# When TensorE reads a tile's expert number, and where VectorE builds the mixer's weights, in a macaron mixture-of-experts and mamba kernel

## The reference, cut to what matters

```
x = x + 0.5 * ffn(layernorm(x))          # x: 16 x 256 tokens of 128
x = x + attn(layernorm(x))
x = x + 0.5 * ffn(layernorm(x))

ffn(x):                                   # 8 experts, top 2, D = 128, H = 512
    probs = softmax(x @ gate_w); vals, idx = top_k(probs, 2); vals /= sum(vals)
    out = sum over e of combine[:, e] * (silu(x @ w1s[e]) @ w2s[e])

attn(x):
    x1 = x + mamba(rmsnorm(x, norm1_w))
    out2 = mamba(rmsnorm(x1, norm2_w))
    return x1 + memory_attend(out2)       # decayed causal reads, chunk 64

mamba(x):                                 # d_inner 256, conv 4, state 16, dt rank 64
    xm, res = split(x @ in_w.T + in_b)
    xm = silu(causal depthwise conv(xm) + conv_b)
    delta, B, C from xm; h = h * exp(delta * A) + delta * xm * B;  y = h . C
    return ((y + xm * D) * silu(res)) @ out_w.T + out_b
```

## Time and profile before

| | us |
|---|---|
| median of 3 runs (1718.62 to 1725.28) | 1719.58 |
| the profiled execution | 1717.3 |
| its span, first to last instruction | 1715.5 |
| TensorE busy (matmul) | 1330.5, 78% |
| VectorE busy | 1379.7, 80% |
| ScalarE busy | 1278.6, 75% |
| GpSimd busy | 568.3, 33% |
| mean granted TensorE clock, share of full speed | 0.901 |

### The profile page before, as it was taken

How to read it: one execution, slowest core, us unless ns; L and a number is a source line. 1 busy time by engine, 2 the same in 40 slices (tenths; PEclk the granted TensorE clock), 3 DMA queues, 4 the chain that set the end, 5 groups by cost and what they waited for, 6 DMA issues and landing times. The chain is left out here.

```text
span 1715.5 us, 29243 instructions
## 1 busy us (share of the span) xinstructions
PE 1330.5 (78%) x8754; PEld 1195.6 (70%) x8754; DVE 1379.7 (80%) x2184; ACT 1278.6 (75%) x2657; POOL 568.3 (33%) x610
## 2 busy tenths in 40 slices
PE   7867667886888788887878788887888688568778
PEld 7756556776767677776767677776777677457668
DVE  2438798989888898989889898989889797978742
ACT  3259765988889797988889697878789688648722
POOL 1211324153341535154342536153342533132220
PEclk9969866998989899998999899998989899768889
DMA  7206545666676766666676766666676765555731
GB/s 243 61 13 154 112 78 129 139 154 141 143 168 152 165 140 161 145 155 143 139 178 148 165 148 159 143 149 140 137 172 148 164 143 112 96 127 116 165 84 47
DMA packets 143510, 234.88 MB, mean 137 GB/s; under 512 B 13568, under 2 KB 79360, under 8 KB 143232
## 3 DMA queue, kind: packets, MB, share of 16 engines
q0 software_dynamic: 39424, 132.15, 39.5%
q1 hardware_dynamic: 103936, 100.87, 20.6%
HBM read 90.36 MB, written 25.17 MB: 67 GB/s over the span
## 5 line engine op out<-in xcount | busy, mean ns | idle before, releaser
L1527 POOL DMA_DIRECT2D acc<-G x224 | 204.2, 912 | 893.0 <-DMA acc<-G 444.5
L934 ACT ACTIVATE dA<-delta,A 128x255 f32<-128x255 f32 x1024 | 425.7, 495 | 4.7 <-DVE hs L1283 3.7
L1302 DVE TENSOR_TENSOR G<-hs,b_r 128x1024 f32<-128x1024 f32 x224 | 272.3, 1216 | 60.4 <-PE b_r L646 53.0
L1289 DVE TENSOR_TENSOR_SCAN hs<-dA,b_r 128x512 f32<-128x512 f32 x256 | 298.2, 1202 | 22.9 <-PE b_r L635 12.5
L1283 DVE TENSOR_TENSOR_SCAN hs<-dA,dbu 128x1024 f32<-128x1024 f32 x128 | 292.7, 2286 | 14.2 <-ACT dA L934 7.7
L540 PE MATMUL b_out<-w2s,hT 128*128 x1680 | 245.7, 292 | 64.9 <-issue 44.2
L540 PEld LDWEIGHTS b_out<-w2s,hT 128*128 128x128 f32 x1680 | 216.2, 201 | 86.3 <-issue 85.3
L528 PE MATMUL b_h<-xsT,wst 128*128 128x128 f32 x1680 | 241.0, 290 | 8.1 <-ACT hT L872 8.1
L813 ACT ACT_TABLE_LOAD x180 | 230.9, 1283 | 3.9 <-PEq L1655 0.7
L528 PEld LDWEIGHTS b_h<-xsT,wst 128*128 128x128 f32 x1680 | 223.9, 207 | 10.6 <-issue 9.9
L950 ACT ACTIVATE scaled<-duT,dtT 128x256 f32<-128x256 f32 x512 | 217.0, 500 | 0.3
(11 more groups left out here) (170 smaller groups left out, 1991.7 us busy)
## 6 DMA issues: line engine op xcount, KB each, us to landing
acc<-G POOLq DMA_DIRECT2D x224, 512.0 KB
wst<-w_dram SPq DMA_DIRECT2D x234, 256.0 KB, 3.0
xsort<-sorted SPq DMA_DIRECT2D x70, 192.0 KB, 5.6
results<-ys SPq DMA_DIRECT2D x70, 192.0 KB, 3.1
xin<-x_dram SPq DMA_DIRECT2D x8, 256.0 KB, 5.3
sorted<-ys SPq DMA_DIRECT2D x2, 960.0 KB, 7.1
sorted<-xn,posi POOLq DMA_INDIRECT x112
yk<-results,posi POOLq DMA_INDIRECT x112, 4.8
```

What stands on the lines that cost most here:

```text
L934: last = do(dA[j % 4][:, d, k, 1:], delta[b][:, k, 1:], ACT.Exp, scale=A[:, k, s:s + 1])
L1289: V.tensor_tensor_scan(hs[j % 2][:, d, :, :].rearrange("p h t -> p (h t)"), dA[j % 4][:, d, :, :].rearrange("p h t -> p (h t)"), R[u % 2][ ...
L1302: V.tensor_tensor(to[:, :, :, :], hs[j % 2][:, :, :, :], both(C).unsqueeze(2).broadcast_to([P, DP, HALVES, T]), ALU.mult).then_inc(q_G, 1)
L1527: Q.dma_start(acc[b][:, :, :, :].rearrange("p d h t -> p (d h t)"), G[j % NG][:, :, :, :].rearrange("p d h t -> p (d h t)"), accum_op=ALU. ...
```

## The change

`ffn_up(n, i)` begins with the `value_load` of tile i's expert and keeps the register in the dictionary `owners`; `ffn_down(n, i)` takes it from there. The number of reads is the same, 210, and SyncE's own reads of `eid` are untouched. `mixer_weights()` is cut into `input_weights(m)`, `selectors()`, `small_weights()` and `set_up()`, which are called after the sums of x = 10, 11, 12, 13 and 14; inside `small_weights()` two drains are merged with others.

```
             def ffn_up(n, i):
                 m = n - 1
+                owners[i] = pe.value_load(eid[m % 2][0:1, i:i + 1], min_val=0, max_val=E - 1)
                 r, k, t = RING_OF["U", i], E + m * NT + i, i % CH * P
                 pe.wait_ge(s_w[k % NW], 16 * (k // NW + 1))
                 wait(pe, f_hact, m * ITEMS + max(r - 1, RING_OF["T", i // CH] + 1))
...
-                e = pe.value_load(eid[m % 2][0:1, i:i + 1], min_val=0, max_val=E - 1)
+                e = owners.pop(i)
                 for c in range(HC):
                     last = mm(Y[:, i % CH * D:(i % CH + 1) * D], hT[i % NH][:, c, :], w2s[:, e, c, :],
...
-            def mixer_weights():
-
-                dve.wait_ge(s_early, 32)
-                for m, nw in enumerate(("norm1", "norm2")):
-                    V.tensor_scalar(inz[:, m, :], win[:, DI:2 * DI], par(nw), None, ALU.mult)
-                    for r in range(DC):
-                        V.scalar_tensor_tensor(out=inx[:, m, r, :], in0=win[:, 0:DI], scalar=par(nw),
-                                               in1=taps[:, r * DI:(r + 1) * DI], op0=ALU.mult, op1=ALU.mult)
+            def input_weights(m):
+                if m == 0:
+                    dve.wait_ge(s_early, 32)
+                nw = ("norm1", "norm2")[m]
+                V.tensor_scalar(inz[:, m, :], win[:, DI:2 * DI], par(nw), None, ALU.mult)
+                for r in range(DC):
+                    V.scalar_tensor_tensor(out=inx[:, m, r, :], in0=win[:, 0:DI], scalar=par(nw),
+                                           in1=taps[:, r * DI:(r + 1) * DI], op0=ALU.mult, op1=ALU.mult)
+
+            def selectors():
+                dve.wait_ge(s_sel, 16 * len(sel_in))
+                for i, b in enumerate(sel_in):
+                    rows = N_SEL // P
+                    V.tensor_copy(selr[:, i * rows:(i + 1) * rows, :], b.rearrange("p (i m) -> p i m", m=P))
+
+            def small_weights():
                 V.tensor_tensor(par("tap_b"), par("tap_b"), win[:, 2 * DI:3 * DI], ALU.mult)
...
+            def set_up():
                 for i in range(4):
                     V.memset(dA[i][:, :, :, 0:1], 0.0)
...
                     elif x == 10:
                         ffn_weights(nx)
-                        mixer_weights()
+                        input_weights(0)
+                    elif x == 11:
+                        input_weights(1)
+                    elif x == 12:
+                        small_weights()
+                    elif x == 13:
+                        selectors()
+                    elif x == 14:
+                        set_up()
```

More of the change, by code:

```diff
@@ L519, in ffn_sorted @@
                 last.then_inc(f_hmm, 1)
+            owners = {}
             def ffn_up(n, i):
                 m = n - 1
+                owners[i] = pe.value_load(eid[m % 2][0:1, i:i + 1], min_val=0, max_val=E - 1)
                 r, k, t = RING_OF["U", i], E + m * NT + i, i % CH * P
@@ L1068, in mixer_weights @@
                                 mybir.AxisListType.X, ALU.add)
[L1069 to L1076, removed]
                 dve.wait_ge(s_Aexp, 1)
@@ L1079, in mixer_weights @@
                 dve.wait_ge(s_set_act, 1)
+                dve.drain()
+                V.tensor_tensor(convb[:, :], tapw[:, :], par("in_b")[:, 0:HALVES], ALU.mult)
                 V.tensor_tensor(MT[:, 0:T], MT[:, 0:T], par("causal"), ALU.mult)
                 dve.drain()
+                V.tensor_tensor(convb[:, :], convb[:, :], par("conv_b"), ALU.add)
                 V.tensor_copy(MT[:, T:T + P], MT[:, 0:P])
```

## The result

The changed kernel takes 1701.7 us (median of 4 runs, 1699.63 to 1705.17), the kernel before 1722.05 beside it (4 runs, 1718.62 to 1725.28): ratio 0.9884, 95% interval 0.9855 to 0.9914. Two more comparisons on other chips gave 0.9869 (0.9828 to 0.9910) and 0.9876 (0.9846 to 0.9907). That is 20 us less, where 10.7 less was forecast. The profiled execution of after is 1702.7 us, its span 1700.9, so the two profiles differ by 14.6; the kernel before varies from run to run (1716 to 1737 on one chip), and its profiled execution was among its fastest.

What follows compares the result with a forecast made beforehand. No engine is full; a chain that changes engine every microsecond or two sets the time. Weights -7.9, read -8.4 + 5.6 = -2.8, together -10.7 us: 1709 us from the median 1719.58, range 1699 to 1719.

Steps and rivals of the forecast that it cites:

- The weights: Last sums of the first FFN: five parts fit VectorE's idle time, saving 7.9 us, 4.9 gap plus 3.0 slow clock.
- What goes, in front of down: Read's stall before the projection down disappears where it is on the path: 0.6 us a layer, 14 layers, 8.4 us.
- The 65 us of idle that could go: TensorE's weight-load idle before down: 99 tiles at 0.66 us each, the upper bound of the gain.
- the share on the path, an eighth: Of 6.1 us idle a layer before down, about an eighth counted as time, from one 0.79 us crossing.
- What comes, in front of up: The read, now before the projection up, is only partly hidden by queued matmuls and adds 5.6 us, bounds 0 and 30.
- the leads of 0.45 and 0.3 us: Sequencer's lead over the array before up, behind a down and behind a `t` step; both shorter than the read's 0.6.
- The 0.4 a layer: New cost before up: two ups right behind a down on the path, at 0.2 us each, 5.6 us in all.
- The free read: Rival: the read costs nothing in front of up because the sequencer's lead carries over; 1703 us, chance 0.22.
- The eaten gain: Rival: 0.3 us more at each of ScalarE's 43 waits for up eats the read's gain and more; 1716 us, chance 0.23.
- the slower case: Rival: the whole 0.7 us is added before up where ScalarE waits for it, +30; 1733 us, chance 0.10.
- the 15 more that were to refute the forecast: Sign: the forecast is wrong if ScalarE's wait for up grows from 57 us by more than 15.

Runs made afterwards that it cites:

- e2: Only the read moved in front of the projection up, weights still in one block, against the kernel before: 1715.06 us, ratio 0.9897.
- e1: Only the weights in five parts, expert still read in front of the projection down, against the kernel before: 1717.78 us beside 1729.96, ratio 0.9931.
- e4: The changed kernel again, unaltered, as yardstick beside the kernel before: 1707.16 us, ratio 0.9869.
- e3: The changed kernel with the read right behind the four matmul calls of the projection up: 1697.56 us, ratio to before 0.9809.
- e6: The changed kernel plus a second read, its value unused, in front of the projection down: ratio to before 0.9992.
- e7: The changed kernel with two reads in front of the projection up, the second's value unused: ratio to before 0.9980.
- e5: The changed kernel with no TensorE read or offset operations, expert from a fixed table, some tiles wrong: ratio to before 0.9817.
- e8: The changed kernel with the weights in two larger parts, after x = 10 and 12, set_up after x = 14: one run, 1705.5 us.

## Why the prediction was right, and where it was too small

- **The weights: right.** 7.9 us forecast, 7.93 between the sums of x = 10 and 15, made of the gap and of the slow matmuls behind it. The granted clock did stay up, and no gap came back. The 3.0 us of slow clock are those of one execution; in e2's it was 1.9, and 6.8 in all. By medians e1 says 12 (8 to 16); the 8 lies at the interval's edge, and what the rest would be is not settled.
- **What goes, in front of down: right place, too small a share.** The 65 us of idle that could go were 67 (85.3 - 17.9). The step that failed is the share on the path, an eighth, for 8.4 us. It was taken from one crossing of 0.79 us in the one layer that the chain of waits reaches. The runs show a quarter: 20 us for 84 us of stall. The crossing itself was read rightly, and the chain of e1, where the read is at the same place, has it too (0.70 us at 1611.55). The chain covers that layer from its first up on (1551.27 in before) and not just its second half, as the prediction says, so the small share is not a half counted as a whole. It is one layer of 14, and no chain shows the others: which crossings make up the rest stays open.
- **What comes, in front of up: right mechanism, too small.** The read did come late for the array there, as the leads of 0.45 and 0.3 us said; up's stall grew by 38 us, and it costs 9 to 12 us where 5.6 were forecast. The 0.4 a layer came from the same one layer, and there the chains of the changed kernel (after and e4) show no stall of 0.1 us or more in front of any up: what it costs is not seen in that layer. The net of the read is thus about 8 to 11 us, and 11 to 18 by e1 and e2, not 2.8; this is most of what the sum missed (10.7 forecast, about 18 with these sizes, 20 measured).
- **The free read.** It was not free in front of up: e3, on the same chip, is 10 us faster. The Trainium skill gives TensorE's queue a depth of 64 ("TensorE: Matmul & The Clock Gate", section "Architectural detail"). A full queue of that depth would have made the read free in front of up, and in front of most downs before; e6 and e7, where one more read costs about 20 and 18 us, show that so much work did not lie ahead of either place. The case's number, 1703, lay nearest to what was measured, but for the wrong reason: it left out the cost in front of up and had too little for the gain in front of down, two errors of opposite sign.
- **The eaten gain and the slower case.** ScalarE's wait for up grew by 9 us in the two profiles (57.1 to 66.0), not by 13 or 30. It is a poor sign of the read: it is 67.0 in e1, where the read was not moved, and 70.5 and 78.1 in e4 and e2, the last over the 15 more that were to refute the forecast. What decides is that e1 against e4 shows a gain of the move as a whole.
- **Two profiles as a measure.** Their spans differ by 14.6, the medians by 20. The forecast was built on one execution of before; it gave the size of the stalls well, but runs of the same kernel on one chip lie up to 20 us apart (1716 to 1737), more than either half of the change.

## What to carry to other kernels

Put a sequencer's read of a register behind a run of queued work that does not need it, not in front of the next one and not in front of its user: the same read cost about 20 and 10 us and nothing measurable at three places a few instructions apart. The lead that covers it can be read off the trace, as the time from a wait that the sequencer passes to the first instruction of the engine behind it. A share read from the chain in one layer of 14 was too small by more than half; a second read put in on purpose at the same place gave the price (e6, e7). For a preparation on an engine that a pipeline waits for, compare each piece with the idle time a stage leaves, and count in the clock that TensorE loses behind a long gap.

## What the runs showed of the hardware

- The read itself takes 0.31 us in the median and up to 1.45. In the profile of before, 126 of the 210 took under 340 ns and 77 over 450. When the slow ones began, 13 packets of GpSimd's software queue were in flight on average, with the fast ones 3 (12 and 2 in the profile of the changed kernel). This was only seen side by side, no run varied it.
- Runs of one program differ, and the slower ones tend to have the lower granted clock: over the 23 runs of before beside e5 to e8 the span goes from 1713.4 to 1733.5 us and the mean granted clock from 0.903 to 0.885, with a correlation of -0.64. In the profiles of before and e1 the lower level lasted 280 and 307 us of 110 to 1530, and e1 took about 20 us longer from the first `delta` on, with the same program. Whether the clock makes a run long, or a run with longer waits has the lower clock, is not shown.
